# Token stage of a two-block audio tower: the projection's bias through TensorE, the second norm through VectorE, and a tile's turn two turns earlier

## What is computed

```python
x = x[:, :n_patch * TIN, :].reshape(bsz, n_patch, TIN * F)   # 1472 rows of 1024
x = layer_norm(x, g1, b1, 1e-6)
x = jnp.einsum('bpd,dh->bph', x, W) + b                      # W: 1024 x 512
return layer_norm(x, g2, b2, 1e-6)                           # h
```

## Time and profile before

| | us |
|---|---|
| median of three runs | 1489.69 |
| the profiled execution | 1490.66 |
| its span in the profile | 1488.9 |
| token stage, first x statistics to last `ln_low` | 7.62 to 142.88 |
| busy over the span: TensorE, VectorE | 1294.1, 916.9 |
| busy over the span: ScalarE, GpSimd | 629.9, 259.4 |

### The profile page before, as it was taken

One profiled execution on the slowest core, in us unless ns is written; L12 is line 12 of the kernel. 1 busy time (PEld: TensorE's weight loads), 2 busy tenths in 40 slices (PEclk: granted clock), 3 DMA queues, 4 the chain that ended last, 5 costly groups with the idle time before them and its releaser, 6 DMA issues.

```text
span 1488.9 us, 30422 instructions
## 1 busy us (share of the span) xinstructions
PE 1294.1 (87%) x10676; PEld 825.1 (55%) x10690; DVE 916.9 (62%) x1918; ACT 629.9 (42%) x1066; POOL 259.4 (17%) x304
## 2 busy tenths in 40 slices
PE   6878899999999999995857999999994888668997
PEld 3436677777777777773524544444442556324443
DVE  5776365556566555658782545555335777688886
ACT  3444444344444434441513444444532333236664
POOL 2444000000000000000002333233335640010000
PEclk9997999999999999997688999999997898789999
DMA  5121343434344343521404776776434640000000
GB/s 184 59 76 43 101 171 136 180 136 184 116 152 170 135 180 136 184 85 43 173 1 154 260 276 235 275 259 228 135 114 124 94 66 3 2 0 8 22 21 32
DMA packets 42703, 184.26 MB, mean 124 GB/s; under 512 B 8688, under 2 KB 9200, under 8 KB 34832
## 3 DMA queue, kind: packets, MB, share of 16 engines
q0 software_dynamic: 19744, 95.41, 19.4%
q1 hardware_dynamic: 19440, 75.41, 14.4%
q10 hardware_dynamic: 3456, 12.58, 2.4%
HBM read 135.65 MB, written 47.73 MB: 123 GB/s over the span
## 4 chain that ended last, share of the span: by engine, by line
PE 56%; DVE 21%; issue 14%; ACT 4%; POOL 2%; DMA 2%; DVEq 1%; ACTq 0%; another core or an unknown queue 0%; POOLq 0%; SPq 0%
PE ps L919 14%; PE ps L921 14%; PE ps L920 14%; PE ps L1026 3%; PE ps L1009 3%; DVE ff L1997 2%; DVE amf L2004 1%; POOL rt_out L472 1%; PE ps L1042 1%; PE ps L1110 1%; PE ps L1343 1%; PE ps L1361 1%; PE ps L1127 1%; DVE nrm L1726 1%; DVE bst L1460 1%
## 5 line engine op out<-in xcount | busy, mean ns | idle before, releaser
L919 PE MATMUL ps<-nT_hi,wa_hi 128*128 128x368 f16 x448 | 148.3, 331 | 11.9 <-DVE wa_lo L1390 8.1
L920 PE MATMUL ps<-nT_lo,wa_hi 128*128 128x368 f16 x448 | 147.9, 330 | 0.0
L921 PE MATMUL ps<-nT_hi,wa_lo 128*128 128x368 f16 x448 | 147.6, 330 | 0.0
L1554 DVE TENSOR_TENSOR a<-sq,E 92x368 f32<-92x368 f32 x64 | 31.7, 535 | 136.3 <-ACT sq L690 136.3
L1726 DVE SCALAR_TENSOR_TENSOR nrm<-ps,xg,nrm 128x256 f32<-128x256 f32 x61 | 29.5, 484 | 133.1 <-ACT nrm L733 110.7
L502 POOL DMA_INDIRECT xg<-xrow,idx x61 | 61.1, 1002 | 276.2 <-PE ps L1110 108.9
L919 PE MATMUL ps<-wa_hi,nT_hi 128*92 128x128 f16 (+1 forms) x560 | 107.9, 237 | 0.0
L920 PE MATMUL ps<-wa_lo,nT_hi 128*92 128x128 f16 (+1 forms) x560 | 107.9, 237 | 0.0
L921 PE MATMUL ps<-wa_hi,nT_lo 128*92 128x128 f16 (+1 forms) x560 | 107.5, 236 | 0.0
L919 PE MATMUL ps<-wide,xT 128*128 x244 | 93.7, 384 | 12.0 <-issue 7.0
L702 ACT ACTIVATE yT_hi<-ps 128x368 f16<-128x368 f32 x64 | 27.9, 475 | 164.9 <-PE ps L1042 164.9
(11 more groups left out here) (308 smaller groups left out, 3340.4 us busy)
## 6 DMA issues: line engine op xcount, KB each, us to landing
we_st<-in_we POOLq DMA_DIRECT2D x16, 1536.0 KB, 6.8
wsp<-we_sp POOLq DMA_DIRECT2D x16, 1536.0 KB, 5.4
wide<-wsp SPq DMA_DIRECT2D x16, 1536.0 KB
yslot<-yt POOLq DMA_DIRECT2D x61, 256.0 KB
wq_st<-in_ffq SPq DMA_DIRECT2D x24, 512.0 KB, 6.2
wq_st<-in_ffq ACTq DMA_DIRECT2D x24, 512.0 KB
wide<-in_wa SPq DMA_DIRECT2D x10, 1024.0 KB, 4.8
xt<-in_x SPq DMA_DIRECT2D x12, 512.0 KB, 3.5
```

The lines of the kernel that those rows point to most:

```text
L919: nc.tensor.matmul(dst, lhs[0], rhs[0], start=start, stop=False)
L920: nc.tensor.matmul(dst, lhs[0], rhs[1], start=False, stop=False)
L921: return nc.tensor.matmul(dst, lhs[1], rhs[0], start=False, stop=stop)
L1554: V.tensor_tensor(B["a"][0:AT, j], B["sq"][0:AT, j], B["E"][0:AT, 2 * j:2 * j + 2].unsqueeze(2).broadcast_to([AT, 2, REP, AT]), ALU.mult). ...
```

## The change

The bias leaves VectorE. `tok_bias` cuts the row `tb`, times 256, into two float16 halves `tbh` on one partition, and moves the copy that makes `onesh` (float16 ones) here from behind the pipeline; `tok_mm` ends its group with two matmuls of one row: ones by `tbh`. So PSUM holds 256 times z with its bias.

The second norm is finished by VectorE. Statistics are read from PSUM (eps times 256 squared); `z_scaled` is (PSUM - mean) times g2, `h_row` is that times the root plus b2, into `h`. ScalarE's `z_norm`, GpSimd's `affine` and one shift are gone.

VectorE's steps are split and interleaved: `Order` gets `mark`, which counts without waiting, and `until`, which waits for such a count later. All steps of z and h now have lag 3, the turn of the tile lag 4, so there are 16 turns, and the gate's logits hang behind turns 13, 14 and 15, and behind the last. The order per turn counts 8.

```diff
+    def mark(self, ins):
+        self.n += 1
+        ins.then_inc(self.sem, 1)
+        return self.n
+
+    def until(self, n):
+        self.eng.wait_ge(self.sem, self.at + n)
...
             pipeline(pool, NT, [(3, root_of(rz_ask, 1, rz_done)), (0, root_of(rx_ask, 0, rx_done)),
-                                (4, root_of(rh_ask, 2, rh_done)), (3, affine)])
+                                (3, root_of(rh_ask, 2, rh_done))])
...
-            pipeline(act, NT, [(1, tok_high), (6, lambda k, p, half: ln_high(k, k, 4 + p)), (0, x_norm), (3, z_norm),
-                               (4, h_norm)], after={0: tok_weights})
+            pipeline(act, NT, [(1, tok_high), (4, lambda k, p, half: ln_high(k, k, 4 + p)), (0, x_norm), (3, h_norm)],
+                     after={0: tok_weights})
...
                 for b in range(KI):
-                    ins = split3(ps[:, 2 + p, :], [A["xT_hi"][:, p, b, :], A["xT_lo"][:, p, b, :]],
-                                 [A["wt_hi"][:, b, :], A["wt_lo"][:, b, :]], b == 0, b == KI - 1)
+                    split3(ps[:, 2 + p, :], [A["xT_hi"][:, p, b, :], A["xT_lo"][:, p, b, :]],
+                           [A["wt_hi"][:, b, :], A["wt_lo"][:, b, :]], b == 0, False)
+                pe.wait_ge(a_tw, 1)
+                for x in range(2):
+                    ins = nc.tensor.matmul(ps[:, 2 + p, :], onesh[0:1, :], A["tbh"][0:1, x, :], start=False, stop=x == 1)
                 ins.then_inc(a_mm, 1)
...
-            pipeline(pe, NT, [(1, tok_turn), (6, lambda k, p, half: ln_turn(k, p, 4 + p)), (2, tok_mm)],
-                     after={0: tok_shift, NT + 2: lambda: gate_logits(0, 5), NT + 3: lambda: gate_logits(5, 10),
-                            NT + 4: lambda: gate_logits(10, 13)})
+            pipeline(pe, NT, [(1, tok_turn), (4, lambda k, p, half: ln_turn(k, p, 4 + p)), (2, tok_mm)],
+                     after={0: tok_shift, NT + 1: lambda: gate_logits(0, 5), NT + 2: lambda: gate_logits(5, 10),
+                            NT + 3: lambda: gate_logits(10, 13)})
...
+                order(V.tensor_copy(onesh[:], ones[:]))
                 order(V.tensor_tensor(A["tb"][:], A["tb"][:], ps[:, 7, :], ALU.add))
+                order(V.tensor_scalar(A["tbh"][0:1, 0, :], A["tb"][0:1, :], WS, None, ALU.mult))
+                V.scalar_tensor_tensor(A["tbh"][0:1, 1, :], A["tb"][0:1, :], WS, A["tbh"][0:1, 0, :], ALU.mult,
+                                       ALU.subtract).then_inc(a_tw, 1)
...
             def z_stats(k, p, half):
                 dve.wait_ge(a_mm, ready(k))
-                z = A["z"][:, p, :]
-                order(V.scalar_tensor_tensor(z, ps[:, 2 + p, :], 1.0 / WS, A["tb"][:], ALU.mult, ALU.add))
+                at[1] = order.mark(stats(ps[:, 2 + p, :], 1, p, 0))
+
+            def z_moments(k, p, half):
+                moments(1, p, 1, rz_ask, 1e-6 * WS * WS)
+
+            def z_scaled(k, p, half):
+
+                dve.wait_ge(rz_done, k + 1)
+                at["z"] = order.mark(V.scalar_tensor_tensor(A["z"][:, p, :], ps[:, 2 + p, :], A["mv"][:, 2 + p, 0:1], A["g2"][:],
+                                                            ALU.subtract, ALU.mult))
+
+            def h_row(k, p, half):
+                order.until(at["z"])
                 dve.sem_inc(a_h, 1)
-                moments(z, 1, p, 1, rz_ask, 1e-6)
+                at["h"] = order.mark(V.scalar_tensor_tensor(row(k), A["z"][:, p, :], rt_out[:, 2 + p:3 + p], A["b2"][:],
+                                                            ALU.mult, ALU.add))
...
-            pipeline(dve, NT, [(3, z_stats), (0, x_stats), (3, shift(1, rz_done, a_sz)), (0, shift(0, rx_done, a_sx)),
-                               (1, x_low), (6, lambda k, p, half: ln_low(k, k, 4 + p)), (4, h_stats),
-                               (4, shift(2, rh_done, ln_st))], order, 7, after={0: tok_weights, 1: tok_bias})
+            pipeline(dve, NT, [(3, z_stats), (0, x_stats(0)), (3, z_moments), (0, x_stats(1)), (0, x_moments), (3, z_scaled),
+                               (0, shift(0, rx_done, a_sx)), (3, h_row), (1, x_low(0)), (3, h_stats), (1, x_low(1)),
+                               (3, h_moments), (4, lambda k, p, half: ln_low(k, k, 4 + p)), (3, shift(2, rh_done, ln_st))],
+                     order, 8, after={0: tok_weights, 1: tok_bias})
```

More of the change, by code:

```diff
@@ L633, in x_norm @@
                                      scale=rt_out[:, p:p + 1]).then_inc(a_norm, 1)
-            def z_norm(k, p, half):
-                act.wait_ge(a_sz, k + 1)
-                nc.scalar.activation(A["z"][:, p, :], A["z"][:, p, :], ACT.Identity, bias=A["nb"][:, 2 + p:3 + p],
-                                     scale=rt_out[:, 2 + p:3 + p]).then_inc(a_zn, 1)
             def h_norm(k, p, half):
@@ L1452, in tok_bias, with stats, moments @@
                 dve.wait_ge(rows_in, 48)
+                order(V.tensor_copy(onesh[:], ones[:]))
                 order(V.tensor_tensor(A["tb"][:], A["tb"][:], ps[:, 7, :], ALU.add))
-            def moments(rows, kind, p, n, sem_out, eps):
+                order(V.tensor_scalar(A["tbh"][0:1, 0, :], A["tb"][0:1, :], WS, None, ALU.mult))
+                V.scalar_tensor_tensor(A["tbh"][0:1, 1, :], A["tb"][0:1, :], WS, A["tbh"][0:1, 0, :], ALU.mult,
+                                       ALU.subtract).then_inc(a_tw, 1)
+            at = {}
+            def stats(rows, kind, p, j):
+                dve.sem_inc(passed, 1)
+                return V.bn_stats(A["bst"][:, 2 * kind + p, j, :], rows)
+            def moments(kind, p, n, sem_out, eps):
                 s = 2 * kind + p
-                dve.sem_inc(passed, 1)
-                for j in range(n):
-                    ins = V.bn_stats(A["bst"][:, s, j, :], rows[:, j * 512:(j + 1) * 512] if n > 1 else rows)
-                order(ins)
+                order.until(at[kind])
                 dve.sem_inc(passed, 1)
@@ L1472, in shift, with x_stats, step, x_moments @@
                 return step
-            def x_stats(k, p, half):
-                dve.wait_ge(x_in[p], 16 * (half + 1))
-                moments(A["xt"][:, p, :], 0, p, 2, rx_ask, 1e-6)
-            def x_low(k, p, half):
-                for j in range(2):
+            def x_stats(j):
+                def step(k, p, half):
+                    if j == 0:
+                        dve.wait_ge(x_in[p], 16 * (half + 1))
+                    ins = stats(A["xt"][:, p, j * 512:(j + 1) * 512], 0, p, j)
+                    if j == 1:
+                        at[0] = order.mark(ins)
+                return step
+            def x_moments(k, p, half):
+                moments(0, p, 2, rx_ask, 1e-6)
+            def x_low(j):
+                def step(k, p, half):
                     dve.wait_ge(a_hi, 2 * k + j + 1)
@@ L1482, in x_low, with h_moments @@
                                     A["xT_hi"][:, p, 4 * j:4 * j + 4, :], ALU.subtract).then_inc(a_lo, 1)
+                return step
             def z_stats(k, p, half):
                 dve.wait_ge(a_mm, ready(k))
[L1486 to L1487 removed]
+                at[1] = order.mark(stats(ps[:, 2 + p, :], 1, p, 0))
[7 more added lines that the diff above has]
+                order.until(at["z"])
                 dve.sem_inc(a_h, 1)
[L1489 removed]
+                at["h"] = order.mark(V.scalar_tensor_tensor(row(k), A["z"][:, p, :], rt_out[:, 2 + p:3 + p], A["b2"][:],
+                                                            ALU.mult, ALU.add))
             def h_stats(k, p, half):
[L1492 to L1499 removed]
+                order.until(at["h"])
+                at[2] = order.mark(stats(row(k), 2, p, 0))
+            def h_moments(k, p, half):
+                moments(2, p, 1, rh_ask, 1e-5)
+            pipeline(dve, NT, [(3, z_stats), (0, x_stats(0)), (3, z_moments), (0, x_stats(1)), (0, x_moments), (3, z_scaled),
+                               (0, shift(0, rx_done, a_sx)), (3, h_row), (1, x_low(0)), (3, h_stats), (1, x_low(1)),
+                               (3, h_moments), (4, lambda k, p, half: ln_low(k, k, 4 + p)), (3, shift(2, rh_done, ln_st))],
+                     order, 8, after={0: tok_weights, 1: tok_bias})
             unit_a_lo(0)
@@ L1505, in _ @@
             order(V.tensor_copy(identh[:], ident[:]))
-            order(V.tensor_copy(onesh[:], ones[:]))
             dve.wait_ge(g_mm, 1)
```

15 lines of the change are left out of this document (2 added, 13 removed).

## The result

Nine runs of the changed kernel beside nine of the kernel before on the same chips: 1477.57 us median (1473.44 to 1483.13) against 1492.14 (1485.26 to 1494.32), ratio 0.9913 [0.9894, 0.9933]. The forecast was 1471 with a range of 1464 to 1481, faster. The profiled execution took 1473.44 us; it is the fastest of its nine, so its 17.2 us less than the profiled execution before (1490.66) flatter the change, and the marks inside the trace are the better measure.

What follows compares the result with a forecast made beforehand. VectorE's in-order queue was taken as the bound, 9.55 us a turn. The stage's end gains 19.4 us, less 0.5 behind it: 18.9, so 1490.66 becomes 1471.8, or 1470.8 against the median: 1471 us, range 1464 to 1481.

Steps and rivals of the forecast that it cites:

- Start and first turn: Before the loop: first z statistics at 34.0 us, then a turn of 7.32 us, so turn 4 begins at 41.3.
- Durations: VectorE's instructions: each new pass 0.67 us until an independent start, 0.99 until a dependent one; statistics from PSUM 0.69.
- VectorE's own turn: Token loop: VectorE's interleaved list takes 7.32 us, 7.38 with the loop's branch, against 9.55 before.
- the loop's branch adds 0.1 every second turn: End of the token loop's body: the jump costs VectorE 0.1 us every second turn, making 7.38 us a turn.
- TensorE's ring: Token loop: path from shift through norm, tile turn and matmuls takes 14.6 us for two turns, 7.3 a turn.
- Drain: Last turns, from turn 12's start: later turns at +7.27 and +13.75, stage end +21.8 to +23.2, +22.4 taken, 122.8 us.
- Behind the stage: After the token stage: TensorE's first projections start about 1.4 us later, up to 1 us lost, 0.5 charged.
- Rival 1: Token loop: interleaving hides less, about 0.6 us a turn returns, 5.4 us, 1476; chance 0.16 with other small losses.
- other small losses: Unspecified small losses, given one shared chance of 0.16 with rival 1.
- Rival 2: Token loop: GpSimd's roots and VectorE's new passes block each other, 9 us, 1480, or 1476 for the second pass; chance 0.07.
- Rival 3: Token stage: TensorE at half clock, n slow matmuls giving 7.3 + 0.216n a turn, up to 1533 us; chance 0.03.
- Rival 4: Behind the token stage: the gain is given back by something running on its own time, about 1488 us; chance 0.04.

Runs made afterwards that it cites:

- grouped: Changed kernel with VectorE's list regrouped: dependent pairs side by side, other work still behind each root request; 8.07 us a turn, ratio 0.9927 to the kernel before.
- no_bias_mm: Changed kernel without the two one-row bias matmuls, so z lacks the projection's bias; ratio 0.9894 to the kernel before.
- old_order: Changed kernel with VectorE's list in the order of before, same instructions and lags, nothing interleaved; ratio 1.0032 to the kernel before.
- branch_moved: Changed kernel with the h shift moved from the end of VectorE's list to its head, lag 4; ratio 0.9903 to the kernel before.
- pool_pass: Changed kernel with one more GpSimd instruction behind the h root in the loop's eight turns, product or memset by turns; ratio 0.9920 to the kernel before.

## Why the prediction was right, and which terms were off

The reasoning held: VectorE's queue set the turn, its waits had work laid into them, GpSimd's passes went for 1.05 us a turn, and the stage's end carried the gain to the row of gates. Step by step:

- *Start and first turn*: 34.19 and 7.39 against 34.0 and 7.32: 0.3 us. That the start fits so well is luck, since the first z statistics scatter from 33.10 to 34.52.
- *Durations*: passes 0.74 and 0.75, as taken; 0.90 from a pass to its dependent one in the drain, 1.00 to 1.03 in grouped's loop (0.99 taken). Statistics from PSUM 0.70 against 0.68 to 0.69 from SBUF; by the Trainium skill ("VectorE: DVE Perf Modes", the TRN2 errata) the difference would be 0.065, and the trace doesn't show it.
- *VectorE's own turn*: 7.36 against 7.32, 0.3 us over the loop. **The step that failed is "the loop's branch adds 0.1 every second turn"**: it adds 0.40 (7.36 and 7.77) at each of the loop's three jumps, and the way out of the loop 0.21, 1.4 us where 0.4 was charged. Before, the branch lay under the shift that GpSimd blocked for 1.2 us; there the turn that holds the jump is the shorter of the two (9.50, the other 9.62). The change took that cover away, and I had read its price where it was hidden.
- *TensorE's ring*: 14.6 taken, 14.93 measured. By the rows: shift done 7.40, 0.14 to the norm, 0.81, 0.06, turn of the tile 0.50, matmuls and pair 5.87, and 0.15 until VectorE starts, the term I left out. It didn't decide the time, for the jump came 0.2 later; with the jump covered it does. The bias pair was charged about right, 0.43, against 0.54 in no_bias_mm.
- *Drain*: turns 13 and 14 at +7.34 and +13.85 (7.27 and 13.75), the last shift at +19.40 (19.47). The end at +23.22 is the upper one of the two given, 22.4 taken: the gate matmuls ran at half clock from about 118.7 on. 0.8 us.
- *Behind the stage*: 0.5 charged, 1.41 lost. The projections started 4.9 us behind the stage's end (125.10 to 130.01) against 4.2 before (142.16 to 146.34): 0.7 later, where 1.4 was forecast. The term that was left out is the clock: 18 of their matmuls now took 0.31 us each, at half clock, against 10 before, 1.1 us more. The cumulative sum waited 1.7 us for them; before, 0.34 us of waiting for VectorE stood there instead.

Together 2.3 us at the stage's end (125.10 against 122.8) and 0.9 behind it, less 0.3 of a shorter transfer: 18.9 forecast, 15.9 at the gate weights. The rest of the span, 1324.7 and 1323.3 us, differs by less than runs of one kernel do; the medians' 14.6 lie within that scatter too.

Rival 1 named the wrong reason: the interleaving hides what it was to hide, 2.0 us a turn, and "other small losses" is what came. Rival 2 didn't come: a root beside the first z pass takes its 0.55 (66.94 to 67.49) and the pass its 0.74. The second z pass, the one that reads two arrays of SBUF, met no root, for it starts 0.36 behind the root's end, so what would happen if they met is not shown here. Rival 3 came in none of the changed kernel's turns in the loop. Its "against" looked at a stretch with 0.99 and missed turns of the kernel before with 0.82 and 0.85; and its sum is too high, for the ring it names holds one tile's matmuls in two turns, so that n slow ones lengthen it by 0.108n a turn, not 0.216n. In old_order, where TensorE was ahead of VectorE, twelve slow matmuls made a turn 1.1 longer. Rival 4 didn't come.

## What to carry to other kernels

An engine's program order is worth measuring on its own: here the moved work and the shorter pipeline were worth nothing with the old list of the same fourteen steps, since each also adds to the fill or to VectorE. Whether the new order alone, in the kernel before, would have won as much was not run. Put work whose operands are long there behind each request and at the place where a loop jumps, and look at what covers a cost before you take its price from a row. And where a serial piece waits for a transfer, lay TensorE's independent products beside it, not ahead of it.

## What the hardware did that I had not expected

- The jump of a loop costs VectorE 0.34 to 0.51 us of idle time when the instruction before it had to wait for a semaphore that came late, and nothing that shows in three other cases: 0.69 us of ready work stands there (branch_moved), a blocked shift stands there (before, pool_pass), or the root came with 1.2 us of work still ahead of the shift (grouped). The ways into and out of the loop left 0.14 to 0.17 (changed kernel and no_bias_mm).
- The z statistics start 0.14 to 0.20 us behind the modelled end of the matmul, wherever they truly wait for it. A row that names TensorE with a lag of 0.32 to 0.36 was not waiting for TensorE.
- Behind 5.6 to 7.0 us without work TensorE's 16 small products took 3.72 us, at half clock, in every kernel that stood idle so long, and 1.97 behind 1.1 to 1.5 us. Between 2.2 and 2.9 us both came: eight transposes took 1.09 us behind 2.88 and 1.97 behind 2.89, in the kernel before. And the clock also fell without any idle time: in the changed kernel's drain it went to half at about 118.7, behind the gate's 8-column matmuls and the turn of a tile, and was back at full for the projections from 135.7 on.
- The transfer of the same row of gates through HBM took 9.0 to 9.9 us from one execution to the next, enough to hide a microsecond gained in front of it.
